# Segment sums of an attention layer: tiles taken in pairs, a start matmul and an accumulating one per pair, one accumulator in SBUF, and addresses that come from a table of pairs

## The chip, the cores and the metric

The kernel runs on one core of a Trainium2 chip. The metric is the device time of one execution in microseconds (us); lower is better. On this core TensorE (PE) multiplies matrices into PSUM, VectorE (DVE), ScalarE (ACT) and GpSimd (POOL) do elementwise work, and SyncE (SP) issues transfers. Each engine has its own instruction queue, shown in the trace as DVEq, ACTq, PEldq and so on, in which waits, register arithmetic and register loads stand between the instructions that do work.

## The reference, cut to what matters

A graph layer over 6250 nodes and 100000 edges, a linear-attention mixer and a mixture of experts. The change concerns the graph attention: a weighted sum of value rows over the edges that end in a node. The edges come sorted by `dst`.

```python
mod_k = K[src] + 0.2 * rel[:, None, :]
scores = jnp.einsum('ehd,ehd->eh', Q[dst], mod_k) / D ** 0.5
seg_max = jax.ops.segment_max(scores, dst, num_segments=N)
ex = jnp.exp(scores - seg_max[dst])
denom = jax.ops.segment_sum(ex, dst, num_segments=N)
w = ex / denom[dst]
agg = jax.ops.segment_sum(w[:, :, None] * V[src], dst, num_segments=N)
```

There are 4 heads of 64 columns, so a value row has 256 float32, and with the 4 exponentials behind it 260 (`AGG`). The kernel sums the exponentials along with the values and divides afterwards.

## The kernel before, in words

The nodes lie in 49 blocks (`RBLK`) of 128. The edges of one block are cut into tiles of 128 edges, one edge per partition; a tile never crosses blocks, and the last tile of a block is padded. There are `T` = 832 places for tiles (104 rows of 8), of which the last are empty.

The stages follow each other, each in a block of its own that all engines enter and leave together:

1. `stage_weights` and `stage_project`: queries, keys and values of all nodes.
2. `stage_tiles`: counts say how many tiles each block has; DVE works out the block of each tile (`M["blk"]`) and its first edge; POOL gathers the edges' data (`t_meta`); DVE writes `M["segment"]` (the node of each edge, -1 for padding) and `t_local` (the node's number within its block), and both kinds are turned by PE so that one edge stands on one partition (`M["src"]`, `M["local"]`).
3. `stage_scores`: in groups of 4 tiles (`GROUP`) POOL gathers key and value rows, SP writes the values to DRAM in tile order (`v_d`, before: 104 rows x 128 partitions x 8 tiles), DVE and PE make the scores.
4. `stage_softmax`: maxima and exponentials on DVE and ACT; ACT also fills the accumulators with zeros (L936).
5. `stage_aggregate`: the stage that the change is about, below.
6. `stage_nodes`, `stage_route`, `stage_experts`: the rest of the layer.

In `stage_aggregate` a group is again 4 tiles. SP loads the values of a group into one of 8 places of `a_v`. ACT copies the exponentials of the group into the last 4 columns of `a_w` (L1087), and multiplies 1 or 2 of the 4 tiles by them, head by head (L1095, four instructions a tile); POOL multiplies the rest in one instruction (L1117). DVE makes the one-hot matrix `a_is_dst` by comparing the row 0..127 (`col`) with each edge's local number (L1135, one instruction for 4 tiles, in `prepare`, two groups ahead), loads the block numbers of the 4 tiles into registers (L1192, L1193), and adds the four results in PSUM to the accumulator at the block's place (L1149, in `add`). Two accumulators take turns, `sums` and `odd_sums`, so that neighbouring adds never touch the same place. PE multiplies each tile's one-hot matrix with its weighted values into a bank of its own (L1182), 8 banks in all. At the end DVE adds the two accumulators (L1167). `a_w` and `a_is_dst` have 4 places (`WRING`).

Nothing schedules this at run time: the order on each engine is that of the code, and semaphores (`summed`, `added`, `ex_ready`, `pool_done`, `act_done`) tie the engines together. `load_row` is a register load and a `snap` of each register.

## Time and profile before

| | |
|---|---|
| time, median of 3 runs | 3004.46 us (3003.83 to 3004.86) |
| the profiled execution, its own time | 2987.19 us |
| its span, first to last instruction | 2985.4 us |
| busy over the span | PE 2223.8 us (74%), DVE 1968.8 (66%), POOL 1479.3 (50%), ACT 822.4 (28%) |
| from the first matmul of the summing stage to its last paired add | 1762.7 to 2227.8 |

The busy shares of the whole span say little here, since each stage has another limit. The stage that the change touches has to be read by its own window: how long one group of four tiles takes, and which engine has no gaps in that time. Names such as `a_w<-a_v` mean that a tile called `a_w` is written from one called `a_v`.

### The profile page before, as it was taken

To read this page: it belongs to the slowest core of one execution; us is meant where nothing else is said; L and a number is where in the kernel's file an instruction comes from. 1 tells how busy PE (TensorE), PEld (TensorE's weight loads), DVE (VectorE), ACT (ScalarE), POOL (GpSimd) and SP (SyncE) were. 2 spreads that over 40 slices of the span, in tenths; PEclk is the share of its full clock that TensorE was granted. 3 is DMA by queue.
4 is the path that set the end of the run, shared out by engine and by line. 5 is a ranking of instruction groups with operands and counts; after the bars stand their busy time and mean duration, and the time that the engine had idled before them with its cause. 6 is when DMAs were issued, how large, how long until landed. Compare 5 with 4: busy or idle time off the path is not lost. (4 is left out here: it accounts for less than half of the span.)

```text
span 2985.4 us, 48886 instructions
## 1 busy us (share of the span) xinstructions
PE 2223.8 (74%) x11266; PEld 1392.2 (47%) x11267; DVE 1968.8 (66%) x3347; ACT 822.4 (28%) x2558; POOL 1479.3 (50%) x1460
## 2 busy tenths in 40 slices
PE   6872667667767666767676749999975999967997
PEld 3441333333333333433333436666654566546886
DVE  6882766766676676767676879999995666541111
ACT  1110110011111001101100177777752555531221
POOL 3555555555555555555555226666645434124442
PEclk9995777777677777777877779999997999988999
DMA  4545878887888787888888737777744435255441
GB/s 149 174 160 167 268 252 259 270 264 250 273 263 254 257 279 255 255 273 263 269 251 270 182 145 232 235 236 235 237 141 152 167 137 178 105 192 185 173 169 55
DMA packets 347414, 636.52 MB, mean 213 GB/s; under 512 B 36018, under 2 KB 224950, under 8 KB 347227
## 3 DMA queue, kind: packets, MB, share of 16 engines
q1 hardware_dynamic: 269259, 373.23, 37.9%
q0 software_dynamic: 77824, 262.55, 27.8%
q8 instruction: 32, 0.52, 0.1%
q14 instruction: 27, 0.22, 0.0%
q10 hardware_dynamic: 272, 0.00, 0.0%
HBM read 461.16 MB, written 175.42 MB: 213 GB/s over the span
## 5 line engine op out<-in xcount | busy, mean ns | idle before, releaser
L690 POOL DMA_INDIRECT s_kv<-kv_d,s_index x832 | 793.0, 953 | 642.2 <-issue 318.1
L821 PE MATMUL s_q_ps<-q,s_is_dst 128*128 x2496 | 511.3, 321 | 406.4 <-DVE s_key L744 304.2
L821 PEld LDWEIGHTS s_q_ps<-q,s_is_dst 128*128 128x128 bf16 x2496 | 210.2, 105 | 569.2 <-issue 503.0
L1182 PE MATMUL a_sum_ps<-a_w,a_is_dst 128*128 128x260 f32 x1664 | 421.4, 397 | 50.2 <-DVE odd_sums L1149 33.6
L740 DVE TENSOR_TENSOR s_key<-s_kv,s_rel_ps 128x1024 f32<-128x1024 f32 x208 | 252.5, 1214 | 222.9 <-remote 217.7
L1117 POOL TENSOR_TENSOR a_w<-a_v,a_w 128x512 f32<-128x512 f32 x208 | 284.7, 1369 | 226.8 <-ACT a_w L1087 172.2
L1182 PEld LDWEIGHTS a_sum_ps<-a_w,a_is_dst 128*128 128x128 f32 x1664 | 300.3, 190 | 171.3 <-DVE odd_sums L1149 125.8
L1095 ACT ACTIVATE a_w<-a_v,a_w 128x64 f32<-128x64 f32 x1248 | 319.9, 335 | 4.7 <-DMA a_v<-v_d 4.6
L826 PE MATMUL s_rel_ps<-rel,s_is_kind 64*128 64x64 bf16 x2496 | 241.6, 207 | 29.0 <-issue 28.8
L749 DVE TENSOR_REDUCE s_part<-s_key 128x16 f32<-128x1024 f32 x208 | 253.8, 1220 | 10.7
L744 DVE TENSOR_TENSOR s_key<-s_key,s_q_ps 128x1024 f32<-128x1024 f32 x208 | 253.9, 1221 | 7.2
L639 ACT COPY scores<-s_part 128x32 f32 (+1 forms) x104 | 22.6, 218 | 834.3 <-issue 665.7
L826 PEld LDWEIGHTS s_rel_ps<-rel,s_is_kind 64*128 64x128 bf16 x2496 | 129.2, 101 | 249.6 <-issue 239.8
L1967 PE MATMUL e_y_ps<-wd,e_ht 128*128 x896 | 203.5, 381 | 11.4 <-ACT e_ht L1919 11.4
L1149 DVE TENSOR_TENSOR sums<-sums,a_sum_ps 128x260 f32 x416 | 175.5, 422 | 37.9 <-issue 21.8
L1601 PE MATMUL h_h_ps<-n_x2t,h_w 128*128 128x512 f32 (+1 forms) x416 | 188.4, 576 | 0.2 <-ACT h_ht L1397 0.2
L707 DVE TENSOR_TENSOR dots<-dots,s_mv_ps 128x512 f32<-128x512 f32 x53 | 36.3, 686 | 222.5 <-remote 222.4
L1967 PEld LDWEIGHTS e_y_ps<-wd,e_ht 128*128 128x128 f32 x896 | 166.0, 190 | 35.1 <-issue 14.7
L1149 DVE TENSOR_TENSOR odd_sums<-odd_sums,a_sum_ps 128x260 f32 x416 | 174.0, 418 | 0.1
L1936 DVE TENSOR_TENSOR e_y<-e_y_ps,bd 128x256 f32<-128x256 f32 x56 | 23.6, 421 | 225.0 <-PE e_y_ps L1967 176.0
L1135 DVE TENSOR_TENSOR a_is_dst<-col,local 128x512 f32<-128x512 f32 x208 | 145.3, 699 | 6.4 <-issue 5.9
L792 PE MATMUL s_mk_ps<-wmix,s_xnt 128*128 128x512 f32 x208 | 134.2, 782 | 0.0
(294 smaller groups left out, 3039.5 us busy)
## 6 DMA issues: line engine op xcount, KB each, us to landing
v_d<-s_kv SPq DMA_DIRECT2D x208, 512.0 KB
a_v<-v_d SPq DMA_DIRECT2D x208, 512.0 KB, 5.3
s_local<-local_d SPq DMA_DIRECT2D x106, 256.0 KB
xh_d<-h_hid SPq DMA_DIRECT2D x24, 1024.0 KB, 7.0
s_kind<-type_d SPq DMA_DIRECT2D x212, 64.0 KB
s_kv<-kv_d,s_index POOLq DMA_INDIRECT x832
kv_d<-pkv SPq DMA_DIRECT2D x50, 256.0 KB, 2.0
wd<-in_L_ffn_Wd SPq DMA_DIRECT2D x8, 1024.0 KB, 12.2
```

The costliest lines, as they stand in the source:

```text
L690: nc.gpsimd.indirect_dma_start(out=kv[:, g * GROUP + b, :], out_offset=None, in_=R["kv"], in_offset=bass.IndirectOffsetOnAxis(ap=index[:, ...
L740: nc.vector.tensor_tensor(by_head(key[:, b]), by_head(kv[:, g * GROUP:(g + 1) * GROUP, 0:C]), rel_ps[b][:, 0:GROUP, None, :].broadcast_to( ...
L744: nc.vector.tensor_tensor(key[:, b], key[:, b], q_ps[b][:], ALU.mult).then_inc(S["qr_free"], 1)
L749: nc.vector.tensor_reduce(part[:, h, b * GROUP:(b + 1) * GROUP, :].rearrange("p u h -> p (u h)"), key[:, b].rearrange("p u (h d) -> p (u h ...
L821: nc.tensor.matmul(q_ps[b][:, u, :], is_dst[:, h, e], M["q3"][:, bass.ds(regs[g % GROUPS * GROUP + u], 1), j, :] .rearrange("p a c -> p (a ...
L826: ins = nc.tensor.matmul(rel_ps[b][:, u, :], is_kind[half, h, u * P:(u + 1) * P], M["rel3"][half, j, :], start=(j == 0), stop=(j == 2))
L1095: ins = nc.scalar.activation(w[:, g % WRING, u, at], v[:, g, u, at], ACT.Copy, scale=w[:, g % WRING, u, C + hd:C + hd + 1])
L1117: nc.gpsimd.tensor_tensor(heads(w[:, at, mine, 0:C]), heads(v[:, g, mine, :]), w[:, at, mine, C:, None].broadcast_to([P, len(tiles), H, D] ...
L1149: nc.vector.tensor_tensor(at, at, sum_ps[g % 2 * GROUP + u][:], ALU.add).then_inc(S["added"], 1)
L1182: ins = nc.tensor.matmul(sum_ps[g % 2 * GROUP + u][:], is_dst[:, g % WRING, u, :], w[:, g % WRING, u, :], start=True, stop=True)
L1601: ins = nc.tensor.matmul(h_ps[c % 2][:, 0:n * P], w1[:, k, c * P:(c + 1) * P], x2t[:, q % 2, 0:n, k * P:(k + 1) * P], start=(k == 0), stop ...
L1967: ins = nc.tensor.matmul(y_ps[n % 2][:, b, :], ht[:, n % 2, c, b * P:(b + 1) * P], M["wd"][:, bass.ds(regs[b], 1), c, :].rearrange("p a n ...
```

## The change

- In `stage_tiles` DVE works out a second table, `items`: one entry for each pair of neighbouring tiles of one block, with the number of the first tile and the block. A block with an odd number of tiles has one pair whose second tile is that of the next block. There are 440 places in it (`ITEMS`), each for 2 tiles. The node numbers are kept whole (`node_of`) and no longer within a block.
- The values in DRAM are kept by partition: 128 partitions x 833 tiles x 256, where a row of a partition is contiguous over all tiles.
- In `stage_softmax` one accumulator is zeroed, in the pieces that the other had; POOL fills `nodes` with the numbers 0..6271 in each partition; SP loads `items`.
- In `stage_aggregate` a group is 2 pairs, and there are 220 groups. SP, ACT and DVE load the numbers of the pairs into registers (SP and ACT one load of two registers a group, DVE three). SP issues two transfers a group (2 tiles each), ACT two copies of exponentials. DVE makes one one-hot matrix a pair, by comparing the block's node numbers with each edge's node, and one add a pair. PE adds both tiles of a pair in one bank. Rows of the neighbouring block's tile match no node of the block. ACT has 2 tiles in every fourth group and 1 in the others. The second accumulator and its last addition are gone.

```diff
 @block.sync (stage_aggregate)
-                    sp.dma_start(v[:, g].rearrange("p u c -> p (u c)"),
-                                 R["v"][bass.ds(i * (VRING // 2) + g // 2, 1)].rearrange("a p n -> (a p) n")
-                                 [:, g % 2 * GROUP * C:(g % 2 + 1) * GROUP * C]).then_inc(v_in[g], 16)
+                    regs = load_row(sp, at_tile, tiles_of(i * VRING + g), T - 2)
+                    for k in range(PAIRS):
+                        sp.dma_start(v[:, g, 2 * k:2 * k + 2, :], R["v"][:, bass.ds(regs[k], 2), :]).then_inc(v_in[g], 16)
 @block.scalar
-        ACT_TILES = {g: range(0, 2 - g % 2) for g in range(VRING)}
+        ACT_TILES = {g: range(0, 2 if g % 4 == 0 else 1) for g in range(VRING)}
+            def copy_scores(n, at):
+                regs = load_row(act, at_tile, tiles_of(n), T - 2)
+                for k in range(PAIRS):
+                    nc.scalar.copy(w[:, at, 2 * k:2 * k + 2, C:], scores[:, bass.ds(regs[k], 2), :]).then_inc(S["ex_ready"], 1)
 @block.vector
+            def ahead(n):
+                return (load_row(dve, tile_at, tiles_of(n), T - 2), load_row(dve, node_at, blocks_of(n), RBLK - 1))
+            def one_hot(at, k, tiles, blocks):
+                nc.vector.tensor_tensor(is_dst[:, at, 2 * k:2 * k + 2, :],
+                                        M["nodes"][:, bass.ds(blocks[k], 1), :].broadcast_to([P, 2, P]),
+                                        node_of[:, bass.ds(tiles[k], 2)][:, :, None].broadcast_to([P, 2, P]),
+                                        ALU.is_equal).then_inc(S["hot_done"], 1)
+                    regs = load_row(dve, sums_at, blocks_of(n), RBLK - 1)
+                    if more:
+                        tiles, blocks = ahead(n + LEAD)
+                    for k in range(PAIRS):
+                        j = n * PAIRS + k
+                        dve.wait_ge(S["summed"], j + 1 + WRING * PAIRS)
+                        dve.wait_ge(S["added"], j + 8)
+                        at = sums[:, bass.ds(regs[k], 1), :].rearrange("p a c -> p (a c)")
+                        nc.vector.tensor_tensor(at, at, sum_ps[(g * PAIRS + k) % 8][:], ALU.add).then_inc(S["added"], 1)
+                        if more:
+                            one_hot((g + LEAD) % WRING, k, tiles, blocks)
-            nc.vector.tensor_tensor(sums[:], sums[:], odd[:], ALU.add).then_inc(S["whole"], 1)
 @block.tensor
+                        for u in range(2):
+                            ins = nc.tensor.matmul(sum_ps[(g * PAIRS + k) % 8][:], is_dst[:, g % WRING, 2 * k + u, :],
+                                                   w[:, g % WRING, 2 * k + u, :], start=(u == 0), stop=(u == 1))
```

How one group stands in DVE's queue inside the loop of `stage_aggregate`. Before (`L1135` is the one-hot matrix, `L1192` and `L1193` the register load and its snaps, `ISA` is register arithmetic for an address or a snap, `L1149` an add):

```order
L1149 TENSOR_TENSOR odd_sums<-odd_sums,a_sum_ps7 128x260
L1135 ISA
L1135 TENSOR_TENSOR a_is_dst<-col,local 128x512
L1192 ISA
L1192 TENSOR_LOAD blk
L1193 ISA
L1146 REGISTER_ALU
L1149 ISA
L1149 TENSOR_TENSOR sums<-sums,a_sum_ps0 128x260
L1146 REGISTER_ALU
```

The same place after the change (`L1080` and `L1081` are the register load and its snaps, `L1222` an add, `L1203` a one-hot matrix of one pair):

```order
L1203 TENSOR_TENSOR a_is_dst<-nodes,node_of 128x256
L1080 ISA
L1080 TENSOR_LOAD items
L1081 ISA
L1080 TENSOR_LOAD items
L1081 ISA
L1080 TENSOR_LOAD items
L1081 ISA
L1219 REGISTER_ALU
L1222 ISA
L1222 TENSOR_TENSOR sums<-sums,a_sum_ps2 128x260
```

Between the last DVE instruction of one group and the first add of the next there was one register load; now there are three, each with its snaps. The `L1080 ISA` ahead of them stands there once in a loop turn of eight groups.

On ACT, one group before (`L1087` the copy of the exponentials, `L1095` the multiplications):

```order
L1087 ISA
L1087 COPY a_w<-scores 128x4x4
L1095 ACTIVATE a_w<-a_v,a_w 128x64 x4
```

and after the change (`L1142` the copies, `L1157` the multiplications):

```order
L1149 ISA
L1080 ISA
L1080 TENSOR_LOAD items
L1081 ISA
L1142 COPY a_w<-scores 128x2x4
L1142 ISA
L1142 COPY a_w<-scores 128x2x4
L1157 ACTIVATE a_w<-a_v,a_w 128x64 x4
```

ACT got a register load ahead of each group's copies, and the copies are two.

## Rows read from the trace of the kernel before

**Rows 1.** Busy time of each engine by stage, the windows in us from the start.

```profile
core 0: us, PE busy (x) PEld busy (x) DVE busy (x) ACT busy (x) POOL busy (x), PEclk, DMA share, GB/s
45.00:225.00 180.00, 137.05 (x452) 77.68 (x452) 150.13 (x432) 30.44 (x92) 102.46 (x186) 0.99 0.50 166
250.00:1705.00 1455.00, 983.77 (x5832) 518.26 (x5832) 979.85 (x1151) 148.73 (x519) 792.98 (x832) 0.74 0.82 258
1762.70:2227.80 465.10, 421.41 (x1664) 300.24 (x1664) 425.48 (x1037) 339.42 (x1445) 283.62 (x207) 1.00 0.70 231
2227.80:2244.40 16.60, 0.00 (x0) 0.00 (x0) 13.43 (x1) 0.00 (x0) 0.00 (x0) 0.58 0.00 0
```

**Rows 2.** Groups of instructions, 1762.7 to 2227.8: count, busy us, mean ns, idle before.

```profile
L1182 PE MATMUL a_sum_ps<-a_w,a_is_dst 128*128 128x260 f32 x1664 | 421.4, 397 | 50.2 <-DVE odd_sums L1149 33.6 <-ACT a_w L1095 8.2
L1095 ACT ACTIVATE a_w<-a_v,a_w 128x64 f32<-128x64 f32 x1240 | 317.9, 335 | 1.2 <-DMA a_v<-v_d 1.0
L1117 POOL TENSOR_TENSOR a_w<-a_v,a_w 128x768 f32<-128x768 f32 x104 | 165.4, 1590 | 103.6 <-ACT a_w L1087 101.2 <-DMA a_v<-v_d 2.0 <-issue 0.4
```

**Rows 3.** Who waited for whom, 1762.7 to 2227.8: us in total, times, longest.

```profile
PEld a_sum_ps L1182 <- DVE odd_sums L1149: 125.8, 206, 1.5
ACT a_w L1087 <- PE a_sum_ps L1182: 113.5, 127, 1.7
DVE sums L1149 <- PE a_sum_ps L1182: 8.9, 3, 8.3
```

**Rows 4.** DVE in order of time, a group within a turn and one across turns.

```profile
2003.45 0.42 DVE L1149 TENSOR_TENSOR odd_sums<-odd_sums,a_sum_ps 128x260 f32 x1
2003.79 0.69 DVE L1135 TENSOR_TENSOR a_is_dst<-col,local 128x512 f32<-128x512 f32 x1
2004.57 0.43 DVE L1149 TENSOR_TENSOR sums<-sums,a_sum_ps 128x260 f32 x1
2004.91 0.42 DVE L1149 TENSOR_TENSOR odd_sums<-odd_sums,a_sum_ps 128x260 f32 x1
...
1980.81 0.42 DVE L1149 TENSOR_TENSOR odd_sums<-odd_sums,a_sum_ps 128x260 f32 x1
1981.46 0.69 DVE L1135 TENSOR_TENSOR a_is_dst<-col,local 128x512 f32<-128x512 f32 x1 [0.23 <-issue]
```

**Rows 5.** Register work in the queues, by line: ns min/median/max, first and last start us.

```profile
L1192 DVEq TENSOR_LOAD <-blk x208: 340/344/611, 1757.2 to 2225.6; - x104
L1192 PEldq TENSOR_LOAD <-blk x52: 1118/2478/4271, 250.6 to 1675.9; - x52
L1192 PEldq TENSOR_LOAD <-expert x14: 332/334/345, 2711.3 to 2948.9; - x14
L1193 DVEq FUSED_REGOPS  x208: 120/148/152, 1757.8 to 2226.0; - x104
L1135 DVEq FUSED_REGOPS  x200: 57/66/106, 1756.9 to 2209.8; - x100
L1149 DVEq FUSED_REGOPS  x832: 57/57/65, 1766.6 to 2227.2; - x167
```

**Rows 6.** PE in order of time: a start, total us, and xcount of matmuls.

```profile
2001.65 2.02 PE L1182 MATMUL a_sum_ps<-a_w,a_is_dst 128*128 128x260 f32 x8 [0.58 <-DVE odd_sums L1149]
```

**Rows 7.** ACT in order of time, within the summing stage.

```profile
2003.85 0.20 ACT L1087 COPY a_w<-scores 128x16 f32 x1 [0.48 <-PE a_sum_ps L1182]
2003.96 1.06 ACT L1095 ACTIVATE a_w<-a_v,a_w 128x64 f32<-128x64 f32 x4
```

**Rows 8.** Issue of the value loads in SP's queue: ns min/median/max.

```profile
L1072 SPq DMA_DIRECT2D a_v<-v_d x208: 332/333/1353, 1756.6 to 2205.1; - x104
```

**Rows 9.** DVE in order of time, in the stage of the tiles.

```profile
236.83 0.84 DVE L491 TENSOR_SCALAR t_src_f<-t_meta 104x1024 f32<-104x1024 int32 x1 [12.78 <-DMA t_meta<-in_edges,t_start_i]
```

**Rows 10.** ACT in order of time, in the softmax stage.

```profile
1729.59 10.80 ACT L936 ACTIVATE sums<-ones 128x12740 f32<-128x12740 f32 x1
1743.88 1.06 ACT L961 ACTIVATE m_score<-m_most 104x1024 f32<-104x1024 f32 x1 [2.54 <-DVE m_most L1026]
```

More of the change, by code:

```diff
@@ L1032, in _, with load_row @@
             dve.wait_ge(S["back"], n_bank)
+def load_row(eng, regs, row, most):
+    eng.load(regs, row)
+    return [eng.snap(r, min_val=0, max_val=most) for r in regs]
 AGG = C + H
@@ L1065, in _, with groups @@
         def _(sp):
-            with sp.Fori(0, TURNS) as i:
-                for g in range(VRING):
+            at_tile = [sp.alloc_register(f"a_sp{k}") for k in range(PAIRS)]
+            def groups(i, count):
+                for g in range(count):
                     for name in ("pool_done", "act_done"):
@@ L1099, in _ @@
             act.wait_ge(S["started"], 1)
-            nc.scalar.copy(w[:, 0, :, C:], M["scores"][:, 0, 0:GROUP * H].rearrange("p (u h) -> p u h", h=H)
-                           ).then_inc(S["ex_ready"], 1)
-            with act.Fori(0, TURNS - 1) as i:
-                groups(i, False)
-            groups(TURNS - 1, True)
+            copy_scores(0, 0)
+            with act.Fori(0, TURNS) as i:
+                groups(i, VRING, False)
+            groups(TURNS, REST, True)
         @block.gpsimd
@@ L1108, in _, with groups @@
             pool.wait_ge(S["started"], 1)
-            with pool.Fori(0, TURNS) as i:
-                for g in range(VRING):
+            def groups(i, count):
+                for g in range(count):
                     n, tiles = i * VRING + g, POOL_TILES[g]
-                    pool.wait_ge(S["ex_ready"], n + 1)
-                    pool.wait_ge(v_in[g], (i + 1) * 16)
+                    pool.wait_ge(S["ex_ready"], (n + 1) * PAIRS)
+                    pool.wait_ge(v_in[g], (i + 1) * (16 * PAIRS))
                     pool.nop(nofuse=True)
@@ L1119, in _ @@
                                             ).then_inc(S["pool_done"], 1)
+            with pool.Fori(0, TURNS) as i:
+                groups(i, VRING)
+            groups(TURNS, REST)
         @block.vector
         def _(dve):
-            nc.vector.memset(is_dst[:, 0, 0, 0:1], 0.0).then_inc(S["added"], 2 * GROUP)
-            for name in ("pool_done", "act_done", "dve_done"):
+            nc.vector.memset(is_dst[:, 0, 0, 0:1], 0.0).then_inc(S["added"], 8)
+            for name in ("pool_done", "act_done"):
@@ L1151, in _ @@
-            at_block = [dve.alloc_register(f"a_at{u}") for u in range(GROUP)]
-            LEAD = 2
-            def groups(i, last):
-                for g in range(VRING):
-                    if not (last and g + LEAD >= VRING):
-                        prepare(i, g + LEAD)
-                    n = i * VRING + g
-                    add(i, g, load_row(dve, at_block, M["blk"][0:1, bass.ds(n * GROUP, GROUP)], RBLK - 1))
-            for g in range(LEAD):
-                prepare(0, g)
-            with dve.Fori(0, TURNS - 1) as i:
-                groups(i, False)
@@ new lines, in one_hot, with groups @@
+            def one_hot(at, k, tiles, blocks):
[3 more added lines that the diff above has]
+                                        ALU.is_equal).then_inc(S["hot_done"], 1)
+            def groups(i, count, last):
+                for g in range(count):
+                    n = i * VRING + g
+                    more = not (last and g + LEAD >= count)
+                    regs = load_row(dve, sums_at, blocks_of(n), RBLK - 1)
[5 more added lines that the diff above has]
+                        dve.wait_ge(S["added"], j + 8)
+                        dve.nop(nofuse=True)
+                        at = sums[:, bass.ds(regs[k], 1), :].rearrange("p a c -> p (a c)")
+                        nc.vector.tensor_tensor(at, at, sum_ps[(g * PAIRS + k) % 8][:], ALU.add).then_inc(S["added"], 1)
+                        if more:
+                            one_hot((g + LEAD) % WRING, k, tiles, blocks)
@@ L1170, in _ @@
+            for g in range(LEAD):
+                tiles, blocks = ahead(g)
+                for k in range(PAIRS):
+                    one_hot(g, k, tiles, blocks)
+            with dve.Fori(0, TURNS) as i:
+                groups(i, VRING, False)
+            groups(TURNS, REST, True)
+            dve.wait_ge(S["added"], ITEMS + 8)
         @block.tensor
@@ L1172, in _, with groups @@
             pe.wait_ge(S["started"], 1)
[L1174 to L1175 removed]
+            def groups(i, count):
+                for g in range(count):
                     n = i * VRING + g
[L1177 removed]
+                    for name in ("pool_done", "act_done"):
                         pe.wait_ge(S[name], n + 1 + VRING)
[L1180 to L1184 removed]
+                    for k in range(PAIRS):
+                        pe.wait_ge(S["hot_done"], n * PAIRS + k + 1)
+                        pe.wait_ge(S["added"], n * PAIRS + k + 1)
+                        for u in range(2):
+                            ins = nc.tensor.matmul(sum_ps[(g * PAIRS + k) % 8][:], is_dst[:, g % WRING, 2 * k + u, :],
+                                                   w[:, g % WRING, 2 * k + u, :], start=(u == 0), stop=(u == 1))
+                        ins.then_inc(S["summed"], 1)
             with pe.Fori(0, TURNS) as i:
[L1187 to L1193 removed]
+                groups(i, VRING)
+            groups(TURNS, REST)
 NQ = NBLK // QUAD
```

151 lines of the change are left out of this document (84 added, 67 removed).

## The prediction

> **What bounds the kernel now.** I read the stages first, by their windows. The summing stage runs from its first matmul at 1762.7 to its last paired add at 2227.8, 465 us for 208 groups of four tiles, 2.24 us a group; the addition of the two accumulators and the leaving of the stage follow, 13.4 us of DVE [rows 1]. Then the waits inside that window: PE's weight loads wait 125.8 us for DVE's adds, ACT's copies 113.5 us for PE, and DVE for PE 8.9 us, nearly all of it once, at the start [rows 3]. So PE waits for DVE, the others wait for PE, and DVE waits for nobody: DVE sets the period. Last, DVE in order of time. Adds start 0.34 us apart, the one-hot matrix 0.34 us behind an add, and the next add 0.78 us behind that, although the matrix takes 0.69 [rows 4]. Four adds and one matrix make 3 x 0.34 + 0.34 + 0.78 = 2.13 us; the turn of the loop, every eighth group, puts 0.65 where 0.34 stood. The reader should see that the 0.78 is not only DVE's arithmetic: meanwhile its queue loads four registers (0.344 us), snaps them (0.148) and computes addresses [rows 5].
>
> **The change, part by part.**
>
> *The two tables.* The second table costs DVE thirteen small instructions in `stage_tiles`. They stand ahead of a wait of 12.78 us for the gathered edges [rows 9]. They are far narrower than the instruction behind that wait (0.84 us for 1024 columns; theirs have at most 196), so at 0.5 us each, an upper bound, they are 6.5 us and hidden. Were that cover gone, they would cost up to those 6.5 us. POOL's fill with node numbers and SP's load of `items` lie beside 51 us of softmax in which nobody waits for either engine. Zero.
>
> *Zeroing.* ACT loses its 10.80 us fill, which ends at 1740.4. By the second exponential ACT waits 2.54 us for DVE [rows 10], so whatever the fill had held up was made good by then, and DVE's chain does not wait for it. I take 0; the 2.54 us bound it.
>
> *The last addition.* 13.4 us of DVE alone, with all other engines idle [rows 1]. It goes in full: -13.4.
>
> *PE.* Eight matmul records a group, 2.02 us for eight [rows 6], of which the last one's own length is about 0.4 [rows 2]: 0.23 apart, so 1.85 us for four tiles. A group keeps four tiles, but there are 220. PE alone would need 407 us.
>
> *ACT.* Multiplications 0.24 us apart (four in 1.06, the last one 0.335 long), 0.11 from a copy to the first [rows 2, 7]. On average 5 multiplications a group (1.20), two copies (0.25), and of the register load with its snaps and addresses, some 0.5, the part that the previous multiplication does not hide, 0.4: about 1.85 us. *POOL:* three tiles in three groups of four, at 1.59 us [rows 2]: at most that. *SP:* two issues at 0.333 [rows 8], one load and its addresses: 1.5 (an estimate). *Transfers:* 512 KB a group at 231 GB/s and a share of 0.70 means 330 GB/s at full share; the projection stage, whose rows in DRAM are 1 to 2 KB, gives 166/0.50 = 332 [rows 1]. Pieces of 2 KB instead of 4 are therefore no dearer, and 220 groups need 350 us. None of these sets the period unless DVE is below 1.9.
>
> *DVE.* Its arithmetic shrinks: two adds and two matrices of 256 columns. An add of 260 columns is followed after 0.34, so each of the four should take 0.34: 1.35 us instead of 2.13. But the queue has to be counted too. From the last add of a group to the first of the next there are 1.12 us (2003.45 to 2004.57) [rows 4]. In them the queue does the matrix's address (0.066), the load's address (0.057), the load (0.344), the snaps (0.148), the add's waits (about 0.06) and its address (0.057) [rows 5]: 0.73. What is left, 0.39 over eight steps, is 0.05 a step (an estimate). After the change the same stretch holds a matrix address from two registers (0.10, the upper end of L1135's), three loads, three snaps of two registers (0.12 each, the lower end of four), the add's waits and address (0.12), and eleven steps (0.55): 1.13 us plus three loads. The rest of the group, first add to matrix to second add, is bound by arithmetic, 2 x 0.335 = 0.67. So a group takes 1.80 us plus three loads, and 0.06 for its share of the loop's turn.
>
> *The price of a load of two registers* is the unknown that decides. No row shows one. Four registers take 0.344 on DVE, 0.086 each; sixteen take at least 1.118 on PE, 0.070 each [rows 5]. A line through both gives 0.21 for two, proportion gives 0.14 to 0.17; a price that does not depend on the number gives 0.344, the upper bound, and PE's sixteen speak against it. Nothing excludes less than 0.14. I take 0.17: 1.86 + 0.51 = 2.37 us a group, 220 x 2.37 = 521 us against 465, +56. The Trainium skill, in "DMA: Bandwidth & Descriptors" (Latency and other measured facts), puts a floor of about 600 ns under such a load; this trace's 208 loads of 0.344 disagree. By that floor a group would take 3.66 us and the stage 805.
>
> *Sum.* +56 for the loop, -13.4 for the last addition, +1 for the first register load ahead of the first transfer: +44 us on the profiled execution's 2987.2 (span 2985.4). That execution lies 17 us under the median of the runs, which I take as an offset: 3004.5 + 44 = **3048 us**.
>
> What waits then: PE for the one-hot matrices and for free banks, ACT and POOL for PE. Pairing halves the adds, and DVE spends the time in its queue.
>
> **Rivals.**
>
> 1. *A load costs the same for two registers as for four.* For it: DVE's and PE's loads of four agree (0.344 and 0.334) [rows 5], as a fixed price would. Against it: sixteen on PE. A group takes 1.86 + 1.03 = 2.89, the stage 636: +158, **3163**. Chance 0.14.
> 2. *The other side: the loads are short.* If two registers take 0.06, a group takes 2.04 and the stage 449: -16 and -13 more, **2976**. The point from which it decides is 478/220 = 2.17 us a group, a load of 0.10. It needs DVE's 0.086 a register to be mostly not per register, or steps under the 0.05 that I estimated: with steps of 0.03 the point moves to 0.18 and my own value would be a tie. At the far end ACT's 1.85 to 1.95 takes over: 429 us, 2956. Chance 0.21.
> 3. *TensorE's clock falls.* PE would be busy 75 to 80% of a group instead of 91%. In the score stage, busy 68% with idle stretches of microseconds, the granted clock was 0.74 on average, a mixture of 1.2 and 2.4 GHz; in the projection, busy 76% with short gaps, it was 0.99 [rows 1]. The gaps here are half a microsecond. If it fell to 0.75, eight matmuls would need 8 x 0.29 = 2.35 on average and up to 3.5 at the low level, a group some 2.8, **3140**. Chance 0.05.
> 4. *The loads of DVE, ACT and SP get in each other's way.* PE's spread from 1.1 to 4.3 us shows that a load can be held up by something; DVE's 0.340 to 0.344 with ACT and SP loading nothing shows no such thing [rows 5]. At PE's median over its minimum, 2.2 times, 0.17 becomes 0.38: a group 3.0, the stage 660, **3187**. Chance 0.05. The 600 ns floor of the Trainium skill's page "DMA: Bandwidth & Descriptors" would end beyond this case, at 3004.5 + 805 - 465 - 12 = 3332; the trace leaves it next to no chance of its own, 0.01, counted here.
> 5. *The score stage*, 1455 us with a DMA share of 0.82 [rows 1], writes the same pieces to another layout. If the writes took longer by 2% of the stage, +15; equally possible below. It widens everything and is no case of its own.
>
> **How the numbers follow.** Forecast 0.55 (3010 to 3095), rivals 0.14, 0.21, 0.05, 0.05. About 0.2% (6 us) is what a measurement of this kernel can tell from no change. The forecast and rival 2 meet there, and I give that strip 0.07: of rival 2 0.03, of the forecast 0.04. Faster 0.18, same 0.07, slower 0.75. For 8 in 10 the range goes from 2975, in the middle of rival 2, to 3155, short of rival 1: some 0.10 below and 0.09 above. The likeliest case's own range is 3010 to 3095.
>
> **What would show it.** Right: between the last one-hot matrix of a group and the next add DVE stands idle for 0.8 us or more with "issue" as the cause, 220 times; DVE's busy share in the stage falls from 91% to 55 to 65%; PE waits for DVE; the two-register load's row reads 0.14 to 0.21. Wrong: the load reads under 0.10, or PE's busy share in the stage stays at 90%; then the period is PE's or ACT's. The last addition's 13.4 us must be gone in any case. A score stage off by more than 5 us would show the layout at work.

## The result and the profile after

| | before | changed |
|---|---|---|
| median of the runs, us | 3004.59 (3003.83 to 3004.86) | 3234.84 (3234.17 to 3239.03) |
| ratio | | 1.0768 [1.0752, 1.0783] |
| profiled execution: span, own time, us | 2985.4, 2987.2 | 3233.1, 3234.9 |
| first matmul to last of the summing stage, us | 463.1 | 702.2 |
| the same, a group of four tiles | 2.23 (208 groups) | 3.19 (220 groups) |

The changed kernel is 230 us slower. The direction was forecast, the size was not: the time lies 80 us above the range. All executions in this document lie close to the others of their kernel but one, 6505 us at a granted clock of 0.402, which is left out. First the summing stage as one window (columns as in [rows 1]).

```profile
1784.70:2488.40 703.70, 487.91 (x1760) 326.33 (x1760) 429.75 (x876) 328.78 (x1526) 305.44 (x219) 0.97 0.51 162
```

The summing stage takes 703.7 us where the kernel before took 465.1 [rows 1]; DVE is busy 429.75 of them, 61%, down from 91%. The 13.43 us of the last addition are gone. The granted clock is 0.97, so TensorE is at its upper level (2.4 GHz) nearly throughout. Then the groups of the profile's page (count, busy us, mean ns, idle before):

```profile
L1222 DVE TENSOR_TENSOR sums<-sums,a_sum_ps 128x260 f32 x440 | 185.3, 421 | 276.6 <-PE a_sum_ps L1249 224.6
L1203 DVE TENSOR_TENSOR a_is_dst<-nodes,node_of 128x256 f32 x440 | 299.8, 682 | 2.7 <-issue 2.7
```

The additions are as long as before (421 ns); the comparisons that make the one-hot matrices have a mean of 682 ns for 256 columns, though the undisturbed ones below take 0.42 us. So two things are to be explained: 277 us of idle DVE in front of the additions, and long comparisons. Who waited for whom in the stage (us in total, times, longest):

```profile
ACT a_w L1142 <- PE a_sum_ps L1249: 357.2, 201, 3.9
PEld a_sum_ps L1249 <- DVE a_is_dst L1203: 329.8, 292, 2.5
DVE sums L1222 <- PE a_sum_ps L1249: 224.6, 139, 5.0
...
DVE sums L1222 <- issue: 51.8, 82, 1.7
```

PE waits for DVE's comparisons, ACT waits for PE, and DVE is said to wait for PE. Such a ring has a cause that this view does not list. It is in the queues, whose loads the next view shows (ns min/median/max, first and last start):

```profile
L1080 DVEq TENSOR_LOAD <-items x660: 518/528/780, 1778.2 to 2486.6; - x165
L1080 SPq TENSOR_LOAD <-items x220: 467/474/690, 1778.0 to 2454.3; - x110
L1080 ACTq TENSOR_LOAD <-items x220: 483/493/697, 1778.1 to 2476.2; - x110
...
L1081 DVEq FUSED_REGOPS  x674: 40/89/120, 1779.0 to 3200.8; - x169
```

A load of two registers takes 0.528 us on DVE. Four took 0.344 [rows 5]. There are 660 of them, 349 us in all. Last, DVE in order of time, and one GpSimd product:

```profile
2100.27 0.42 DVE L1222 TENSOR_TENSOR sums<-sums,a_sum_ps 128x260 f32 x1 [0.54 <-issue]
2100.61 0.42 DVE L1203 TENSOR_TENSOR a_is_dst<-nodes,node_of 128x256 f32 x1
2100.95 0.42 DVE L1222 TENSOR_TENSOR sums<-sums,a_sum_ps 128x260 f32 x1
2101.28 0.42 DVE L1203 TENSOR_TENSOR a_is_dst<-nodes,node_of 128x256 f32 x1
2103.38 0.42 DVE L1222 TENSOR_TENSOR sums<-sums,a_sum_ps 128x260 f32 x1 [1.69 <-issue]
2103.73 1.12 DVE L1203 TENSOR_TENSOR a_is_dst<-nodes,node_of 128x256 f32 x1
...
2103.09 1.47 POOL L1178 TENSOR_TENSOR a_w<-a_v,a_w 128x768 f32<-128x768 f32 x1 [3.65 <-ACT a_w L1142]
```

A group takes 3.11 us (2100.27 to 2103.38). Between its last addition (2100.95) and the next (2103.38) lie 2.43 us, of which its three loads (0.529 to 0.542 each) are 1.60. The comparison at 2103.73 takes 1.12 us; a GpSimd product runs from 2103.09 to 2104.56, and the comparison ends 0.29 us after it. Of the 440 comparisons of the trace 119 are over 0.47 us, and each of these began while a product ran and ended 0.28 us after it.

### The profile page after: what moved, and what is told of

It is laid out like the page before. It is cut to its first block and busy times, and to the rows that moved or that the text cites. A ratio compares the mean times of both kernels' runs of the same rounds, so it can differ in the third digit from the quotient of the medians.

```text
span 3233.1 us, 51131 instructions
## 1 busy us (share of the span) xinstructions
PE 2295.4 (71%) x11362; PEld 1420.5 (44%) x11363; DVE 1966.9 (61%) x3201; ACT 801.8 (25%) x2642; POOL 1510.6 (47%) x1474
## 5 line engine op out<-in xcount | busy, mean ns | idle before, releaser
L1249 PE MATMUL a_sum_ps<-a_w,a_is_dst 128*128 128x260 f32 x1760 | 487.9, 416 | 223.1 <-DVE a_is_dst L1203 213.8
L1178 POOL TENSOR_TENSOR a_w<-a_v,a_w 128x512 f32<-128x512 f32 x220 | 306.6, 1394 | 441.0 <-ACT a_w L1142 386.8
L1249 PEld LDWEIGHTS a_sum_ps<-a_w,a_is_dst 128*128 128x128 f32 x1760 | 326.4, 199 | 384.6 <-DVE a_is_dst L1203 329.8
L1222 DVE TENSOR_TENSOR sums<-sums,a_sum_ps 128x260 f32 x440 | 185.3, 421 | 276.6 <-PE a_sum_ps L1249 224.6
L1203 DVE TENSOR_TENSOR a_is_dst<-nodes,node_of 128x256 f32 x440 | 299.8, 682 | 2.7 <-issue 2.7
L1157 ACT ACTIVATE a_w<-a_v,a_w 128x64 f32<-128x64 f32 x1100 | 285.7, 335 | 3.6 <-DMA a_v<-v_d 3.6
L1142 ACT COPY a_w<-scores 128x8 f32 x440 | 66.3, 197 | 367.7 <-PE a_sum_ps L1249 357.2
```

Of the source, the lines that this page charges most:

```text
L1157: ins = nc.scalar.activation(w[:, g % WRING, u, at], v[:, g, u, at], ACT.Copy, scale=w[:, g % WRING, u, C + hd:C + hd + 1])
L1178: nc.gpsimd.tensor_tensor(heads(w[:, at, mine, 0:C]), heads(v[:, g, mine, :]), w[:, at, mine, C:, None].broadcast_to([P, len(tiles), H, D] ...
L1203: nc.vector.tensor_tensor(is_dst[:, at, 2 * k:2 * k + 2, :], M["nodes"][:, bass.ds(blocks[k], 1), :].broadcast_to([P, 2, P]), node_of[:, b ...
L1249: ins = nc.tensor.matmul(sum_ps[(g * PAIRS + k) % 8][:], is_dst[:, g % WRING, 2 * k + u, :], w[:, g % WRING, 2 * k + u, :], start=(u == 0) ...
```

## The experiments

They came in three batches, and each ratio is to the kernel before in the same batch: 3001.9 us (2996.2 to 3004.7, 13 runs), 2616.8 (2613.8 to 2617.1, 7) and 2616.4 (2611.4 to 2617.9, 7). In the second and third the kernel before was 385 us shorter. In every kernel of these two the score stage ends at 1333 to 1336 us, where it ended at 1706 to 1723 in the first; its transfers moved 346 GB/s instead of the 258 of [rows 1]; why is open. The summing stage of before differed by 4 us (459.3 against 463.1), so I compare stages, from the start of the first matmul to the start of the last.

**Load sizes, first try.** Sixty loads of other sizes on DVE, their registers not used.

```diff
+            for _ in range(6):
+                dve.load(probe[0:1], row[0:1, 0:1])
+                dve.load(probe[0:2], row[0:1, 0:2])
...
```

> The kernel before, with 60 register loads more on VectorE's queue ahead of the summing loop: six times each of 1, 2, 2 (from place 1), 2 (from place 2), 3, 4, 4 (from place 2), 4 (from place 1), 8 and 16 registers from the block table; their values are not used. The changed kernel's loads of two registers take 0.528 us, those of four 0.344 before. Theory A (the number and placing of the registers makes the price, whatever the table): two registers read 0.5 us or more here too. Theory B (the price comes from the new table, or from three engines loading side by side): two read 0.34 or less here, and the price grows with the number.

3001.36 us, and none of the sixty has a record in the trace: nothing follows for the price. They took no time that shows either: from the first record of the softmax stage to the first matmul of the summing stage it is 56.5 us here and 56.3 in the kernel before. The run serves for something else, as its kernel is in effect the one before. Its summing stage:

```profile
L1195 PE MATMUL a_sum_ps<-a_w,a_is_dst x1664: 382/382/797, 1776.6 to 2239.7; 128*128 128x260 f32 x185
```

463.1 us, as in the profile of before, but it starts 14 us later. The score stage had already ended 14 us later (the softmax stage's first record is at 1720.13, against 1706.35 in the profile of before), and the loads stand behind it: the stages ahead differ by that much from one execution to another with no edit in them.

**The kernel before with two loads of two.**

```diff
-   add(i, g, load_row(dve, at_block, M["blk"][0:1, bass.ds(n * GROUP, GROUP)], RBLK - 1))
+   add(i, g, load_row(dve, at_block[0:2], M["blk"][0:1, bass.ds(n * GROUP, 2)], RBLK - 1)
+       + load_row(dve, at_block[2:4], M["blk"][0:1, bass.ds(n * GROUP + 2, 2)], RBLK - 1))
```

> The kernel before, but DVE loads the four block numbers of a group in two loads of two registers. Queue theory with the changed kernel's price (two loads at 0.53, each with its snaps and steps, in the place of 0.344 and 0.148): the stretch from the last add to the next first add grows from 1.12 to about 1.95, 208 groups make +170 us, near 3175. If two registers cost 0.17 to 0.21 here: +0.05 to +0.15 a group, 3015 to 3035. If the queue did not bound the stage: no change, 3004.

3171.69 us, ratio 1.0572 [1.0555, 1.0590]. Load and comparison (ns min/median/max):

```profile
L1193 DVEq TENSOR_LOAD <-blk x416: 523/529/798, 1766.0 to 2405.2; - x139
...
L1135 DVE TENSOR_TENSOR a_is_dst<-col,local x208: 684/1289/1881, 1765.4 to 2399.8; 128x512 f32<-128x512 f32 x104
```

Without pairs, tables or loads on other engines, splitting one load costs 170 us: the price is in the load of two. 2 x 0.529 - 0.344 = 0.71 us a group explains 149 us of it. The second load's own snaps, address and steps add some more: in the group whose last addition starts at 2000.62 the comparison (1.24 us) is over when the next addition starts at 2002.53, 1.91 us later, where the kernel before has 1.12; 208 times that difference would be 164 of the 170 us. The comparisons are stretched too, 202 of 208 over 0.75 us against 4 in the kernel before, but in 131 of 205 groups they end before the next addition starts. What they cost of the remaining 6 us no run separates.

**The layout of the value rows alone.** The kernel before with value rows kept by partition.

```diff
-         "v": dram("v_d", (TS_ROWS, P, TS_COLS * C)), ...
+         "v": dram("v_d", (P, T + 1, C)), ...
```

> The kernel before, with the values in DRAM kept by partition (a row pitch of 833 KiB) as in the change, but still one transfer of four tiles a group without registers. The changed kernel's profile has its score stage end 16.6 us later than that of before. Theory that the layout costs this: +14 to +17 us, 3019 to 3021, and the score stage longer by as much than in the run of before beside it. Rival, that the score stage only differs from execution to execution: 3004, within 0.2%.

2999.75 us (10 runs), ratio 0.9994 [0.9984, 1.0004]. The layout costs nothing. Its summing stage starts 14 us later than the one in the profile of before, within 0.2 us of the run with the unused loads, which has the old layout:

```profile
L1181 PE MATMUL a_sum_ps<-a_w,a_is_dst x1664: 382/382/794, 1776.8 to 2240.2; 128*128 128x260 f32 x185
```

**GpSimd's node numbers later.** In the changed kernel GpSimd's fill starts after DVE's first eight steps of the softmax stage.

```diff
+            pool.wait_ge(S["steps"], 8)
             nc.gpsimd.iota(M["nodes"]...
```

> The changed kernel, with POOL's fill of node numbers held back until DVE's eighth step of the softmax stage, behind its seven wide comparisons and scalings. Port theory (the DVE instruction that takes 5.89 us instead of 0.74 waits for POOL's fill of 5.74): it is back at 0.74 and the time falls by 5 us, to 3230. If DVE's scans behind are held up instead: no gain, 3235.

3223.44 us (three executions), ratio 1.0741 [1.0720, 1.0763]. That interval overlaps the changed kernel's, so the total alone does not settle it; the rows do. First the changed kernel's softmax stage in order of time, then the same instruction here.

```profile
1722.98 0.53 POOL L920 MEMSET x_pairs<- 128x512 f32 x1 [32.43 <-POOLq L581]
...
1725.45 5.74 POOL L925 IOTA nodes<- 128x6272 f32 x1
...
1725.85 5.89 DVE L1025 TENSOR_SCALAR m_in_last<-segment 104x1024 f32<-104x1024 f32 x1
```

```profile
1719.46 0.74 DVE L1026 TENSOR_SCALAR m_in_last<-segment 104x1024 f32<-104x1024 f32 x1
...
1721.67 5.36 POOL L926 IOTA nodes<- 128x6272 f32 x1 [2.68 <-DVE m_in_last L1028]
```

One comparison over 1024 columns takes 5.89 us beside the 5.74 us fill and 0.74 when the fill comes later. From the first record of the softmax stage to the first matmul of the summing stage the changed kernel takes 61.7 us and this one 56.5, so the prediction's "nobody waits for either engine" was wrong by 5 us.

**Load sizes, each register used.** The kernel before with forty loads ahead of the summing stage; each loaded register is the address of a vector instruction, so the loads stay.

```diff
+            def try_load(first, count):
+                for r in load_row(dve, probe[0:count], M["blk"][0:1, first:first + count], RBLK - 1):
+                    nc.vector.tensor_tensor(sums[:, bass.ds(r, 1), :], ...).then_inc(S["whole"], 1)
+            for _ in range(4):
+                for first, count in ((0, 1), (1, 1), (0, 2), (1, 2), (0, 3), (0, 4), (2, 4), (0, 5), (0, 6), (0, 8)):
+                    try_load(first, count)
```

> The kernel before, with forty more loads into VectorE's registers at the head of the summing stage: one, two, three, four, five, six and eight neighbouring numbers of the table of blocks, at two offsets for one, two and four; each loaded register is then used as the address of a vector instruction on the (still zero) sums, which changes nothing in them. It measures the disputed price by itself. Theory (the price of a load depends on how many registers it fills, and two are dearer than four): the rows of two registers read 0.52 to 0.53 us, those of four 0.34. Rival (two in the loop were dear for what stood around them: a moving address, other engines' loads): the rows of two read 0.34 or less here. A third reading, that the price goes by whether the numbers start at a multiple of their own length, would part the two offsets from each other. The whole takes some 100 us longer than the kernel before; the total decides nothing.

2723.54 us in a single execution, with the forty loads and what uses them in it; the rows are what counts. Eight loads of the third round, each by its line in a window of its own. In order: one register; two; three; four from the first number of the table; four from its third number; five, six and eight from the first.

```profile
L1204 DVEq TENSOR_LOAD <-blk x1: 313/313/313, 1444.8 to 1444.8; - x1
L1204 DVEq TENSOR_LOAD <-blk x1: 539/539/539, 1446.7 to 1446.7; - x1
L1204 DVEq TENSOR_LOAD <-blk x1: 746/746/746, 1450.2 to 1450.2; - x1
L1204 DVEq TENSOR_LOAD <-blk x1: 359/359/359, 1452.8 to 1452.8; - x1
L1204 DVEq TENSOR_LOAD <-blk x1: 968/968/968, 1455.6 to 1455.6; - x1
L1204 DVEq TENSOR_LOAD <-blk x1: 618/618/618, 1459.1 to 1459.1; - x1
L1204 DVEq TENSOR_LOAD <-blk x1: 821/821/821, 1462.7 to 1462.7; - x1
L1204 DVEq TENSOR_LOAD <-blk x1: 605/605/605, 1467.3 to 1467.3; - x1
```

The price falls from three registers (0.746) to four (0.359), and is 0.968 for four that start at the table's third number. The other rounds agree, but for the very first load of all (0.556 for one register). Two from an odd place took 0.529, as from an even one. The numbers fit one reading: 0.31 for a single number and 0.21 to 0.26 for each further one, while four that start at a multiple of four count as one piece of 0.35, and a further piece of four adds 0.25. By it eight are 0.60 (0.605 measured), five 0.35 + 0.23 = 0.58 (0.618), six 0.35 + 2 x 0.23 = 0.81 (0.821), and four out of place 0.31 + 3 x 0.22 = 0.97 (0.968). Sixteen are 0.35 + 3 x 0.25 = 1.10; PE's shortest was 1.118 [rows 5]. Four registers were tried from two places only, so that the piece must start at a multiple of four is this reading, not a measurement of every place.

The same trace by windows, the score stage and the summing stage, shows what differs between the batches and what does not:

```profile
250.00:1340.00 1090.00, 910.96 (x5852) 503.54 (x5853) 980.91 (x1161) 154.03 (x524) 795.12 (x835) 0.82 1.02 346
1502.00:1961.70 459.70, 421.61 (x1664) 300.35 (x1664) 422.07 (x1035) 336.36 (x1432) 274.42 (x204) 1.00 0.70 225
```

**Three loads of four.** The changed kernel, its table stored by group, each of DVE's three loads fetching four numbers, of which it uses two.

```diff
-        item_i = sb("t_item_i", [IT_ROWS, 2, IT_COLS], I32)
+        item_i = sb("t_item_i", [IT_ROWS, IT_COLS // 2, 2, 2], I32)
+        row_of = lambda n: items[0:1, bass.ds(n * 4, 4)]
+            def load_four(regs, n, first, most):
+                dve.load(regs, row_of(n))
+                return [dve.snap(r, min_val=0, max_val=most) for r in regs[first:first + 2]]
```

> The changed kernel with its table stored by group (two tile numbers, then two block numbers), and each of VectorE's three loads a group made into a load of all four numbers, of which it uses two. Same number of loads, same uses; SyncE's and ScalarE's loads still fill two registers. Theory (the count of registers sets the price): the three loads take 0.344 in place of 0.528 each, a group goes from 3.11-3.20 to about 2.6 us, total 3235 - 220 x 0.55 = about 3110. Rival (each load has a floor of about 0.53 whenever three are issued in a row or the table is this one): rows stay at 0.53, total stays at 3235. If the one-hot comparisons' wait for GpSimd (0.26 us each in the changed kernel) comes to light once the queue is shorter, a group takes up to 0.3 us more: up to 3180.

2723.76 us, ratio 1.0414 [1.0397, 1.0432].

```profile
L1201 DVEq TENSOR_LOAD <-items x660: 336/344/607, 1387.8 to 1974.9; - x165
...
L1254 PE MATMUL a_sum_ps<-a_w,a_is_dst x1760: 382/382/799, 1394.3 to 1975.5; 128*128 128x260 f32 x196
```

Loading twice as many registers takes 121 us off the stage: 581.2 us, 2.64 a group in place of 3.19 (2.6 was expected), and three times 0.184 is 0.55. Without its loads a group takes 3.19 - 3 x 0.528 = 1.61 there and 2.64 - 3 x 0.344 = 1.61 here. So the price of the loads is the whole difference between the two, and the fixed part is the same.

**One load of four.**

```diff
+            row_at = [[dve.alloc_register(f"a_row{b}_{k}") for k in range(4)] for b in range(4)]
+            def ahead(n, g):
+                at = row_at[g % 4]
+                dve.load(at, row_of(n))
+                return limit(at[0:2], T - 2), limit(at[2:4], RBLK - 1)
-                    regs = load_row(dve, sums_at, blocks_of(n), RBLK - 1)
+                    regs = limit(row_at[g % 4][2:4], RBLK - 1)
```

> The changed kernel with the table stored by group and one load of four registers a group on VectorE in place of three loads of two: the block numbers stay in their registers (four sets in turn) until the addition of their group, two groups later. GpSimd's fill with node numbers waits until VectorE's first wide steps are done. SyncE's and ScalarE's loads fill two registers as in the changed kernel. Theory A (VectorE's queue alone sets the period): 1.50 us of work and turn, 0.344 for the load and 0.1 for the register copies make 1.95 us a group, then ScalarE at 1.85 to 2.1 is next: stage 430 to 460 us, total 3235 - 10 - 704 + 430 to 460 = 2950 to 2980, below the kernel before. Theory B (a one-hot comparison and a GpSimd product exclude each other): two comparisons of 0.42 and a product of 1.35 on average make at least 2.19 us a group, stage 482 or more, total 3003 or more, and the trace shows most comparisons stretched to 0.7 us and above with GpSimd's product beside them.

This kernel, and the later ones built on it, also hold back GpSimd's fill as above.

2639.39 us, ratio 1.0090 [1.0074, 1.0107]; stage 502.8 us. DVE and GpSimd in order of time:

```profile
1599.62 0.41 DVE L1208 TENSOR_TENSOR a_is_dst<-nodes,node_of 128x256 f32 x1
...
1600.29 1.35 DVE L1208 TENSOR_TENSOR a_is_dst<-nodes,node_of 128x256 f32 x1
1601.56 0.41 DVE L1227 TENSOR_TENSOR sums<-sums,a_sum_ps 128x260 f32 x1
1601.90 1.67 DVE L1208 TENSOR_TENSOR a_is_dst<-nodes,node_of 128x256 f32 x1
1603.49 0.41 DVE L1227 TENSOR_TENSOR sums<-sums,a_sum_ps 128x260 f32 x1
...
1599.73 1.63 POOL L1180 TENSOR_TENSOR a_w<-a_v,a_w 128x768 f32<-128x768 f32 x1 [0.65 <-ACT a_w L1144]
1601.82 1.47 POOL L1180 TENSOR_TENSOR a_w<-a_v,a_w 128x768 f32<-128x768 f32 x1 [0.46 <-ACT a_w L1144]
```

Theory B, within its numbers (2.29 us a group against 2.19 or more). The loads are out of the way, and DVE is still late: 218 of 440 comparisons are stretched. The one at 1601.90 ends at 1603.57; the product at 1601.82 ends at 1603.29, 0.28 us earlier. The one before it ended at 1601.64, and the product beside it at 1601.36, 0.28 us earlier again. It goes the other way too: the product at 1599.73, which started while the comparison at 1599.62 ran, took 1.63 us in place of 1.47. The additions between, which read one input from PSUM, keep their 0.41. The Trainium skill, in "SBUF — State Buffer" (Who interferes with whom), describes a port pair that VectorE and GpSimd share under an exclusive lock, and counts a tensor_tensor with both inputs in SBUF among what needs it; these rows agree.

**Loads of four on SyncE and ScalarE too.**

```diff
-                regs = load_row(act, at_tile, tiles_of(n), T - 2)
+                regs = load_row(act, at_tile, row_of(n), T - 2)
```

> As the kernel with one load of four on VectorE, and SyncE's and ScalarE's loads a group fill four registers too (two used): 0.34 in place of 0.47 and 0.49. If ScalarE sets the period there, a group is 0.15 us shorter, 33 us over the stage. If comparisons against GpSimd or VectorE's queue set it, the time is within 5 us of the kernel with one load on VectorE alone.

2631.22 us, ratio 1.0056 [1.0039, 1.0073].

```profile
L1254 PE MATMUL a_sum_ps<-a_w,a_is_dst x1760: 382/382/772, 1390.7 to 1886.3; 128*128 128x260 f32 x196
...
L1081 SPq TENSOR_LOAD <-items x220: 294/300/513, 1384.3 to 1864.5; - x110
L1081 ACTq TENSOR_LOAD <-items x220: 304/308/526, 1384.3 to 1878.2; - x110
```

Those loads fall from 0.47 and 0.49 to 0.30 and 0.31 us, the stage by 7 us to 495.6 and the total by 8. The 33 us that a stage bound by ScalarE would have given did not come, so ScalarE was not the limit; the 7 us are a little more than the 5 that I allowed, and what gave them no run separates.

**The comparison reads PSUM.** The column numbers stand in a PSUM bank; the block's first node is added as a scalar. Four banks hold the sums.

```diff
-                nc.vector.tensor_tensor(is_dst[:, at, 2 * k:2 * k + 2, :],
-                                        M["nodes"][:, bass.ds(blocks[k], 1), :].broadcast_to([P, 2, P]),
-                                        node_of[:, bass.ds(tiles[k], 2)][:, :, None].broadcast_to([P, 2, P]),
-                                        ALU.is_equal).then_inc(S["hot_done"], 1)
+                nc.vector.scalar_tensor_tensor(out=is_dst[:, at, 2 * k:2 * k + 2, :],
+                                               in0=col_ps[:, None, :].broadcast_to([P, 2, P]),
+                                               scalar=M["nodes"][:, bass.ds(blocks[k], 1), 0:1]...,
+                                               in1=node_of[:, bass.ds(tiles[k], 2)][:, :, None].broadcast_to([P, 2, P]),
+                                               op0=ALU.add, op1=ALU.is_equal).then_inc(S["hot_done"], 1)
```

> The kernel with loads of four everywhere, in which the one-hot comparison no longer reads a 128-wide row of node numbers from SBUF: the numbers 0 to 127 stand in one PSUM bank, a block's first node is added as a scalar, and the sum is compared with the tile's node numbers (one instruction of VectorE, 256 wide, one wide input from PSUM). Four PSUM banks hold the pair sums in place of eight. Theory (a comparison with both inputs in SBUF and a GpSimd product exclude each other): with the wide input in PSUM the comparisons are no longer stretched, one takes 0.49 (an instruction of that kind and width elsewhere in the kernel takes 0.485) in place of 0.86 on average, and a group goes from 2.26 to 2.05 to 2.15 us: from the first to the last matmul 450 to 475 us in place of 495.6, total 25 to 45 us less, 0.99 of the kernel before. Rival (the stretch comes from any SBUF traffic of VectorE beside GpSimd, or from the queue): comparisons still take 0.8 us and above on average, and with 0.07 us more each the stage is 495 to 530 us.

2554.68 us (2554.17 to 2555.14), ratio 0.9766 [0.9750, 0.9783]: **faster than both kernels**. The stage by window, the comparison's line and PE's wait for it:

```profile
1392.20:1809.40 417.20, 405.50 (x1760) 318.97 (x1760) 338.72 (x875) 326.96 (x1526) 298.02 (x219) 0.99 0.84 274
...
L1211 DVE SCALAR_TENSOR_TENSOR a_is_dst<-a_col_ps,nodes,node_of x440: 474/479/484, 1386.7 to 1807.3; 128x256 f32<-128x256 f32 x147
...
PE a_sum_ps L1258 <- DVE a_is_dst L1211: 11.5, 25, 0.5
```

All 440 comparisons lie between 474 and 484 ns. The stage is 416.8 us, 1.89 a group; PE is busy 405.50 of 417.20 and waits 11.5 us for comparisons, so TensorE is now the bound. The stage is 33 us below the 450 that I gave as its lower end. The edit changes the kind of instruction as well as where its wide input lies, and no run separates the two; that the place decides is supported by the additions, of the same kind as the old comparisons but with one input in PSUM, none of which is over 0.43 us beside a product.

**GpSimd's product cut to one tile.** In the kernel with loads of four everywhere. The kernel leaves out the products of the other one or two tiles, whose buffers are zeroed once ahead of the stage.

```diff
-                    n, tiles = i * VRING + g, POOL_TILES[g]
+                    n, tiles = i * VRING + g, POOL_TILES[g][:1]
```

> The kernel with loads of four everywhere, in which GpSimd multiplies only the first of its two or three tiles of a group; the products of the others are left out (their buffers are zeroed once before the stage, some 5 us). Theory (exclusion): GpSimd is busy for 0.5 us a group in place of 1.4, so most comparisons fall to 0.42 us, and the stage falls from 495.6 to some 430 to 455 us, where VectorE's own queue or ScalarE is next. Rival (VectorE's queue, ScalarE or PE sets 2.26 us already): the stage stays within 10 us of 495.6.

2554.95 us, ratio 0.9770 [0.9754, 0.9786].

```profile
1395.70:1809.10 413.40, 401.69 (x1760) 318.65 (x1760) 336.95 (x875) 326.96 (x1526) 159.40 (x219) 1.00 0.85 277
...
L1210 DVE TENSOR_TENSOR a_is_dst<-nodes,node_of x440: 410/420/879, 1390.3 to 1807.0; 128x256 f32 x147
```

Cutting GpSimd's time from 308 to 160 us gives what reading PSUM gives, within 4 us of the stage. The 79 to 83 us (495.6 against 416.8 and 412.9) were the price of the two engines keeping each other out, or the part of it that shows before TensorE's own 402 to 406 us bound the stage.

**Four banks alone,** the control for the comparison from PSUM.

```diff
-        sum_ps = [... for b in range(8)]
+        sum_ps = [... for b in range(4)]
```

> A control for the comparison from PSUM: the kernel with loads of four everywhere, with four PSUM banks for the pair sums in place of eight and nothing else changed. A bank is free two groups after its addition rather than four; if that costs nothing, the stage is 495.6 us within 5 from the first matmul to the last.

2633.77 us, ratio 1.0067 [1.0050, 1.0084].

```profile
L1254 PE MATMUL a_sum_ps<-a_w,a_is_dst x1760: 382/383/771, 1391.3 to 1886.9; 128*128 128x260 f32 x196
```

495.6 us, the same as with eight.

**The changed kernel with GpSimd's product cut to one tile.** The same edit in the changed kernel, which leaves out the same products.

> The changed kernel itself (three loads of two registers) with GpSimd multiplying only the first tile of its two or three in a group; the products of the others are left out. Theory (in the changed kernel the loads in VectorE's queue set the period, and the stretch of the comparisons lies under them for the greater part): from 702.2 us the stage falls by 20 to 30 us, to the 3.11 us a group of an undisturbed group. Rival (the exclusion is a cause of its own size, 0.26 us on each of 440 comparisons): the stage falls by 80 to 116 us.

2849.34 us, ratio 1.0891 [1.0873, 1.0909], 233 us above before as the changed kernel was 230.

```profile
L1251 PE MATMUL a_sum_ps<-a_w,a_is_dst x1760: 382/383/772, 1400.4 to 2102.1; 128*128 128x260 f32 x196
...
L1205 DVE TENSOR_TENSOR a_is_dst<-nodes,node_of x440: 410/419/875, 1395.5 to 2100.5; 128x256 f32 x147
...
L1080 DVEq TENSOR_LOAD <-items x660: 518/528/785, 1393.8 to 2101.8; - x165
```

701.7 us against 702.2. Shorter comparisons (mean 0.49 in place of 0.68) give nothing back, not even the 20 us that my theory allowed. In the changed kernel the queue with its 0.528 us loads sets the period, and the exclusion lies under it: what it costs there is too small to see.

## Why the prediction was wrong in size and right in sign

**The bound and the engine.** Right. DVE set the period and its queue, not its arithmetic, does so after the change.

**The price of a load of two registers.** This is the step that failed: "A line through both gives 0.21 for two, proportion gives 0.14 to 0.17; a price that does not depend on the number gives 0.344, the upper bound". It measured 0.528, above the bound. I had taken for granted that a load of fewer registers is never dearer. The two rows that I drew the line through, four and sixteen, are both whole pieces of four; nothing between them was known. Three loads at 0.36 more than taken are +1.07 us a group, 236 us.

**The fixed part.** 1.80 us and 0.06 for the turn were taken, 1.61 measured. From the last addition to the next, less the loads, 2.43 - 1.60 = 0.83 us were needed where I had 1.13: the snaps of two registers took a median of 0.089 instead of 0.12, and the queue's steps lie some 0.035 apart where I had 0.05. That is -0.25 us a group, -55 us. Both together: 2.37 + 1.07 - 0.25 = 3.19, the measured period.

**The rest of the sum.** From matmul to matmul the stage grew by 702.2 - 463.1 = 239.1 us. The last addition gave its 13.4 back, as forecast. GpSimd's fill, taken at zero, cost 5. The score stage ended 16.6 us later in this profile (the first record of the next stage is at 1722.98, against this one of the kernel before); two kernels with and without the new layout show 14 of that as difference between executions.

```profile
1706.35 0.53 POOL L879 MEMSET x_pairs<- 128x512 f32 x1 [36.55 <-POOLq L542]
```

239.1 - 13.4 + 5 + 16.6 = 247.3, and the spans differ by 247.7. The 17 us by which the profiled execution of before lay under its median, and which the forecast took as an offset, are most likely the same thing, as the changed kernel's profiled execution has no such offset (3234.9 against a median of 3234.84): without them 239.1 - 13.4 + 5 = 231, and the medians differ by 230. The tables' own instructions and the zeroing show nowhere in this account, as forecast.

**The rivals.** A fixed price (1) would have given 2.89 us a group; the price is not fixed but falls at four. Short loads (2), the other side, did not happen. The clock (3) stayed at 0.97. That loads of three engines get in each other's way (4) is excluded by the kernel before with two loads of two: 0.529 with nothing loading beside it. The floor of about 600 ns, of the Trainium skill's "DMA: Bandwidth & Descriptors" (Latency and other measured facts), is not borne out: one, two and four registers took 0.31, 0.53 and 0.36. Layout (5): nothing, ratio 0.9994. In rival 3 the product 8 x 0.29 is 2.32 and not 2.35, which changes nothing.

**The range.** By the prediction's own chances rivals 1 (3163) and 4 (3187), 0.19 together, lie above 3155; it counted 0.09 there. A range for 8 in 10 should have reached past rival 1. It would still have missed, as no rival had a load of two dearer than 0.38 us but the floor of 600 ns, which had 0.01.

**What was to show.** DVE's busy share of 55 to 65% (61), PE waiting for DVE, and the long idle stretch before a group's first addition came. The profile put most of that stretch down to PE rather than to "issue", which is where the last signal came from; the loads stand only in the queue's rows. The load's own row, 0.14 to 0.21 expected, told the miss at once.

**What was overlooked.** That a comparison with both inputs in SBUF cannot run beside a GpSimd product. In the kernel before the two fitted: 0.70 us of comparison and 1.37 of product in 2.23, with 4 of 208 comparisons stretched. In the changed kernel it is hidden. It is worth 79 to 83 us once each engine makes one load of four a group.

## What to carry to other kernels

Lay out tables of addresses so that one load fetches a whole aligned piece of four numbers, keep the numbers in registers until their last use, and fetch four even where two are needed: here 0.344 us against 0.528. When a group of instructions is short, look at the queue's rows as well as the waits. Price register loads by a row of the same count and place; a line between two counts can be wrong in sign. When VectorE and GpSimd share a stage, add up VectorE's instructions with both inputs in SBUF and GpSimd's time: where the sum comes near the period, give one of VectorE's inputs a place in PSUM.

## What the runs showed of the hardware

- A register load on VectorE: 0.31 us for one number, 0.53 for two, 0.75 for three, 0.36 for four in place, 0.97 for four out of place, 0.62, 0.82 and 0.60 for five, six and eight (one execution, four rounds); in the loops 0.528 for two and 0.344 for four. On ScalarE two take 0.493 and four 0.308, on SyncE 0.474 and 0.300.
- VectorE and GpSimd: a comparison of 256 columns with both inputs in SBUF that starts beside a running product ends 0.28 us after it, up to 1.7 us long, and a product that starts beside a running comparison is held up in the same way (1.63 us in place of 1.47); a TENSOR_SCALAR over 1024 columns took 5.89 us beside a 5.74 us fill, 0.74 otherwise. With the wide input from PSUM none of 440 comparisons was over 0.484 us.
- Sixty loads whose registers nobody uses left no record in the trace and took no time that shows.
